# A fused patch, attention and expert kernel with its head rebuilt: gamma and beta spread by TensorE, attention weights first

## The reference

```python
parts = [x] + [_shift2d(x, HALF * s[2], HALF * s[0]) for s in shifts]
xc = jnp.concatenate(parts, axis=1)                      # 15 channels
patches = ... .reshape(B, h * w, p * p * C5)             # 3840 features a patch
mu = patches.mean(axis=-1, keepdims=True)
var = patches.var(axis=-1, keepdims=True)
xn = (patches - mu) * jax.lax.rsqrt(var + LN_EPS) * ln_gamma + ln_beta
return jnp.einsum('bnp,dp->bnd', xn, W) + b              # W: 192 x 3840
```

## Time and profile before

| | us |
|---|---|
| median of 3 runs | 677.99 (677.66 to 678.62) |
| the profiled execution, whole | 683.48 |
| its span in the profile | 681.7 |
| PE busy in the span | 543.7 (80%) |
| DVE, ACT, POOL busy | 406.0, 300.6, 198.3 |

### The profile page before, as it was taken

One profiled execution on the slowest core, in us unless ns is written; L12 is line 12 of the kernel. 1 busy time (PEld: TensorE's weight loads), 2 busy tenths in 40 slices (PEclk: granted clock), 3 DMA queues, 4 the chain that ended last, 5 costly groups with the idle time before them and its releaser, 6 DMA issues.

```text
span 681.7 us, 13237 instructions
## 1 busy us (share of the span) xinstructions
PE 543.7 (80%) x3330; PEld 504.9 (74%) x3331; DVE 406.0 (60%) x1343; ACT 300.6 (44%) x696; POOL 198.3 (29%) x293
## 2 busy tenths in 40 slices
PE   0079989997699999997019999999999999999300
PEld 0067688997497788886019999999999999999300
DVE  4590717666314789999715656565665656565297
ACT  0035991223523677876314444444544444444100
POOL 0001510000000267777702333333333333333300
PEclk9999997999579999998559999999999999999855
DMA  9999600000951022222222322222222222222398
GB/s 201 236 173 187 120 0 1 7 1 0 225 159 36 22 73 74 82 78 81 78 77 52 82 68 80 69 80 69 69 80 72 77 68 81 68 80 61 107 373 259
DMA packets 85235, 64.87 MB, mean 95 GB/s; under 512 B 42500, under 2 KB 81896, under 8 KB 84824
## 3 DMA queue, kind: packets, MB, share of 16 engines
q1 hardware_dynamic: 67160, 39.93, 26.4%
q0 software_dynamic: 8208, 16.95, 6.9%
q10 hardware_dynamic: 9840, 7.67, 3.9%
HBM read 42.61 MB, written 21.86 MB: 95 GB/s over the span
## 4 chain that ended last, share of the span: by engine, by line
PE 65%; DVE 15%; ACT 8%; DMA 6%; issue 3%; SPq 2%; ACTq 1%; POOL 0%; POOLq 0%; DVEq 0%
PE pair L736 9%; PE bank L931 5%; PE bank L927 5%; PE bank L928 4%; PE bank L930 4%; PE bank L929 4%; PE bank L938 4%; DVE hres L1334 4%; ACT sqjunk L463 4%; PE pair L947 4%; PE bank L947 4%; DMA bet<-in_L_tok_ln_beta 3%; PE pair L916 3%; PE pair L806 3%; PE bank L687 3%
## 5 line engine op out<-in xcount | busy, mean ns | idle before, releaser
L648 POOL DMA_INDIRECT disp<-xf,posu x82 | 79.7, 972 | 166.6 <-DVE posu L1212 142.0
L660 POOL DMA_INDIRECT ydram<-ysb,dnow x89 | 87.3, 981 | 69.4 <-POOL dnow L657 67.1
L1310 DVE TENSOR_TENSOR hh<-sg,bank 128x384 f32<-128x384 f32 x89 | 49.3, 554 | 84.0 <-ACT sg L601 84.0
L601 ACT ACTIVATE sg<-bank 128x384 f32<-128x384 f32 x89 | 43.7, 491 | 110.9 <-PE bank L931 110.9
L736 PE MATMUL pair<-wcT,imgT 128*128 128x193 f32 x432 | 74.7, 335 | 3.3 <-DVE tmp L1048 3.3
L736 PEld LDWEIGHTS pair<-wcT,imgT 128*128 128x128 f32 x432 | 73.7, 196 | 3.5 <-issue 3.5
L927 PE MATMUL bank<-wa,xh 128*128 x178 | 67.5, 379 | 0.0
L931 PE MATMUL bank<-wa,xl 128*128 x178 | 60.0, 337 | 0.0
L928 PE MATMUL bank<-wa,xh 128*128 x178 | 60.0, 337 | 0.0
L929 PE MATMUL bank<-wa,xl 128*128 x178 | 59.8, 336 | 0.0
L930 PE MATMUL bank<-wa,xh 128*128 x178 | 59.7, 335 | 0.0
(11 more groups left out here) (229 smaller groups left out, 1258.0 us busy)
## 6 DMA issues: line engine op xcount, KB each, us to landing
xs<-disp SPq DMA_DIRECT2D x89, 96.0 KB, 2.0
img<-in_x SPq DMA_DIRECT2D x12, 392.0 KB, 8.3
yall<-ydram SPq DMA_DIRECT2D x5, 768.0 KB, 13.9
yall<-ydram ACTq DMA_DIRECT2D x5, 768.0 KB, 15.0
hres<-in_txt SPq DMA_DIRECT2D x4, 768.0 KB, 13.2
xs<-disp SPq DMA_DIRECT2D x89, 33.5 KB, 1.9
wraw<-in_L_tok_W SPq DMA_DIRECT2D x1, 2880.0 KB, 17.0
raw_gu<-in_L_ffn_gate_w SPq DMA_DIRECT2D x7, 288.0 KB, 10.7
```

The costliest lines, as they stand in the source:

```text
L648: pool.indirect_dma_start(disp, bass.IndirectOffsetOnAxis(ap=posu[c % XBUF][:, 2 * j + k:2 * j + k + 1], axis=0), xfd[c % XBUF][:, j, :], None
L660: pool.indirect_dma_start(ydram, bass.IndirectOffsetOnAxis(ap=dnow[b][:], axis=0), ysb[b][:], None).then_inc(s_ys[b], 16)
L1310: v.tensor_tensor(hh[o][:], sg[o][:], bank[2 * o + 1][:, 0:DE], ALU.mult).then_inc(s_hh, 1)
```

## The change

- `gamma` and `beta` come as one row each into `gb1` on one partition. PE multiplies them by a column of ones (`onesf`, K = 1) in 8 pieces of 480 columns each, and ACT copies each piece from PSUM to `gam` or `bet` (`spread(n)`, 16 pieces, four banks). Pieces 0 to 7 stand first in PE's and ACT's streams, pieces 8 to 15 behind the 16 attention products.
- SP now issues gamma, beta, the four attention weights, `wraw` in two halves and the image. ACT issues only the constants and small parameters.
- The products use four banks; ACT copies `gT`, DVE copies `hT`.
- DVE zeroes nothing of the image any more (POOL does), makes the small tables and centres `wq` first, and then waits for all 16 spread pieces before the gamma multiply, which goes to a new tile `wsc`. The folds are made in `wsc`, counted by `s_wsc`; PE's weight transposes wait for them alone. The beta sums come after the folds.
- POOL waits for `s_wprep` and cuts strips 0, 2, 4, 5, 6, 7; DVE cuts 1 and 3 (`strip_out`).
- Of image groups 0 to 15 DVE copies the even ones and ACT the odd ones. ACT's eight copies stand ahead of `squares(0)`.
- `patch_out(p)` waits for `s_sq` at 2p+2 and no longer for 18.
- The text load is split in two (after the weight transposes, after the squares), and the groups of `stats1` are in another order.

```diff
         @block.sync
-            sp.dma_start(wraw[:], W.rearrange("(m p) f -> p m f", p=DH)).then_inc(s_wraw, 16)
-            sp.dma_start(bet[:], beta.partition_broadcast(DH)).then_inc(s_bet, 16)
-            sp.dma_start(gam[:], gamma.partition_broadcast(DH)).then_inc(s_gam, 16)
+            for k, w in enumerate((gamma, beta)):
+                sp.dma_start(gb1[:, PFEAT * k:PFEAT * k + PFEAT], w.unsqueeze(0)).then_inc(s_gb, 16)
+            sp.dma_start(wq[:], w_query.rearrange("(c p) d -> p c d", p=P)).then_inc(s_attw, 16)
...
+            for m in range(2):
+                sp.dma_start(wraw[:, m, :], W[DH * m:DH * m + DH, :]).then_inc(s_wraw[m], 16)
...
         @block.scalar
+            def spread(n):
+                act.wait_ge(s_gbm, n + 1)
+                to = (gam, bet)[n // 8]
+                nc.scalar.copy(to[:, 480 * (n % 8):480 * (n % 8) + 480], bank[4 + n % 4][0:DH, 0:480]).then_inc(s_gbo, 1)
...
-            act.wait_ge(s_wprep, 1)
+            for g in range(1, 16, 2):
+                act.wait_ge(s_it, g + 1)
+                nc.scalar.copy(imgT[:, g // 4, g % 4, :, :], bank[3 + g % 2][:, 0:CH * P].rearrange("p (c t) -> p c t", c=CH)
+                               ).then_inc(s_ita, 1)
...
         @block.gpsimd
+            pool.wait_ge(s_wprep, 1)
             pool.wait_ge(s_img, 16 * 12)
             pool.wait_ge(s_border, 1)
-            for r in range(8):
+            for r in (0, 2, 4, 5, 6, 7):
...
         @block.tensor
+            def spread(n):
+                if n >= 4:
+                    pe.wait_ge(s_gbo, n - 3)
+                pe.matmul(bank[4 + n % 4][0:DH, 0:480], onesf[:], gb1[:, 480 * n:480 * n + 480], start=True, stop=True
+                          ).then_inc(s_gbm, 1)
...
-            pe.wait_ge(s_wprep, 1)
+            for n in range(8, 16):
+                spread(n)
+            pe.wait_ge(s_wsc, 8)
             for g in range(12):
...
         @block.vector
+            v.wait_ge(s_gbo, 16)
+            for m in range(2):
+                v.wait_ge(s_wraw[m], 16)
+                st.link(v.tensor_tensor_reduce(wsc[:, m, :], wraw[:, m, :], gam[:], 1.0, 0.0, ALU.mult, ALU.add,
+                                               colsum[:, 0, m:m + 1]))
...
+            for m in range(2):
+                st.link(v.tensor_tensor_reduce(wraw[:, m, :], wraw[:, m, :], bet[:], 1.0, 0.0, ALU.mult, ALU.add,
+                                               colsum[:, 1, m:m + 1]))
...
             def patch_out(p):
-                v.wait_ge(s_sq, 18)
+                v.wait_ge(s_sq, 2 * p + 2)
...
+            strip_out(1)
+            for g in range(0, 16, 2):
+                if g == 8:
+                    strip_out(3)
                 img_out(g)
```

More of the change, by code:

```diff
@@ L304, in part_of @@
             return (1 if s == 0 else 3) if dr <= 0 else (4 if s == 0 else 2)
-        wv5 = wraw[:].rearrange("p m (y x c) -> p m y x c", y=16, x=16)
+        wv5 = wsc[:].rearrange("p m (y x c) -> p m y x c", y=16, x=16)
         def pipeline(eng, step, parts, ahead, peel=0):
@@ L362, in _ @@
                                      x[:, c, 40 * ih:40 * ih + 56, 40 * jh:40 * jh + 56]).then_inc(s_img, 16)
-            sp.wait_ge(s_wprep, 1)
+            sp.wait_ge(s_wt, 12)
             for q in range(TQ):
-                sp.dma_start(hres3[32 * q:32 * q + 32, PTILES:TILES, :], txt_q[q]).then_inc(s_txt, 16)
+                sp.dma_start(hres3[32 * q:32 * q + 32, PTILES + 8:TILES, :], txt_q[q][:, 8:]).then_inc(s_txt[0], 16)
+            sp.wait_ge(s_sq, 18)
+            for q in range(TQ):
+                sp.dma_start(hres3[32 * q:32 * q + 32, PTILES:PTILES + 8, :], txt_q[q][:, 0:8]).then_inc(s_txt[1], 16)
             sp.wait_ge(s_it, 32)
@@ L629, in _ @@
                                pattern=[[1, P]], channel_multiplier=-1).then_inc(s_cons, 1)
+            for ih in range(2):
+                pool.wait_ge(s_pool, 4 + 3 * ih)
+                pool.memset(img[64 * ih:64 * ih + 64, :, 56 * ih:56 * ih + 8, :], 0.0).then_inc(s_pool, 1)
+                for jh in range(2):
+                    a, r0 = 64 * ih + 32 * jh, 8 - 8 * ih
+                    pool.wait_ge(s_pool, 5 + 3 * ih + jh)
+                    ins = pool.memset(img[a:a + 32, :, r0:r0 + 56, 56 * jh:56 * jh + 8], 0.0)
+                    if not (ih and jh):
+                        ins.then_inc(s_pool, 1)
+            ins.then_inc(s_border, 1)
+            pool.wait_ge(s_wprep, 1)
             pool.wait_ge(s_img, 16 * 12)
             pool.wait_ge(s_border, 1)
-            for r in range(8):
+            for r in (0, 2, 4, 5, 6, 7):
                 if r >= 2:
@@ L670, in _ @@
         def _(pe):
+            def spread(n):
[3 more added lines that the diff above has]
+                          ).then_inc(s_gbm, 1)
+            pe.wait_ge(s_pool, 1)
+            pe.wait_ge(s_gb, 32)
+            for n in range(8):
+                spread(n)
             pe.wait_ge(s_cons, 1)
@@ L683, in _ @@
                 h, o = n // 2, 64 * (n // 2 % 2)
-                pe.wait_ge(s_eg, n + 1 if n else 2)
+                pe.wait_ge(s_ega, 2)
+                if n >= 4:
+                    pe.wait_ge(*((s_egd, (n - 3) // 2) if n % 2 else (s_ega, n // 2 + 1)))
                 lhs, rhs = (wk, wq) if n % 2 == 0 else (wv, woT)
                 for m in range(2):
-                    ins = pe.matmul(bank[n % 2][0:DH, D * m:D * m + D], lhs[o:o + 64, h // 2, DH * m:DH * m + DH],
+                    ins = pe.matmul(bank[n % 4][0:DH, D * m:D * m + D], lhs[o:o + 64, h // 2, DH * m:DH * m + DH],
                                     rhs[o:o + 64, h // 2, :], start=True, stop=True)
                 ins.then_inc(s_pg, 1)
-            pe.wait_ge(s_wprep, 1)
+            for n in range(8, 16):
+                spread(n)
+            pe.wait_ge(s_wsc, 8)
             for g in range(12):
                 if g == 0:
-                    pe.wait_ge(s_eg, 2 + 2 * NH)
+                    pe.wait_ge(s_ega, 2 + NH)
+                    pe.wait_ge(s_egd, NH)
                 if g >= 2:
@@ L718, in img_t @@
             def img_t(g):
-                if g >= 2:
-                    pe.wait_ge(s_itout, g - 1)
+                if 2 <= g < 18:
+                    pe.wait_ge((s_itd, s_ita)[g % 2], g // 2)
+                elif g >= 18:
+                    pe.wait_ge(s_itd, g - 9)
                 r, m = g // 4, g % 4
-                pe.wait_ge(s_strip, r + 1)
+                if r in (1, 3):
+                    pe.wait_ge(s_strip1, r // 2 + 1)
+                else:
+                    pe.wait_ge(s_strip, r // 2 + 1 if r < 4 else r - 1)
                 for c in range(CH):
@@ L728, in patch @@
                 i, j = p // 3, p % 3
-                pe.wait_ge(s_itout, min(32, 8 * i + 16))
+                pe.wait_ge(s_itd, 8 * i + 8)
+                pe.wait_ge(s_ita, 8)
                 if p == 0:
@@ L961, in _ @@
             st = Steps(v, s_dve)
[L963 to L1000, removed]
             v.wait_ge(s_rw8, 32)
@@ L1015, in _ @@
             st.mark(v.memset(zrow[:], 0.0))
+            v.wait_ge(s_attw, 64)
+            st.link(v.tensor_reduce(wqm[:], wq[:], AX.X, ALU.add))
+            st.link(v.tensor_scalar(wqm[:], wqm[:], 1.0 / D, None, ALU.mult))
+            v.tensor_tensor(wq[:], wq[:], wqm[:].unsqueeze(2).to_broadcast([P, 4, D]), ALU.subtract).then_inc(s_wqc, 1)
+            for n in range(1, 2 * NH, 2):
+                v.wait_ge(s_pg, n + 3)
+                v.tensor_copy(hT[:, :, n // 2, :], bank[n % 4][0:DH, 0:384].rearrange("p (m d) -> p m d", m=2)
+                              ).then_inc(s_egd, 1)
+            v.wait_ge(s_gbo, 16)
[4 more added lines that the diff above has]
+            for m in range(2):
+                for dr in range(2):
+                    for s in range(2):
+                        px, ox = (8, 0) if s == 0 else (0, 8)
+                        y0 = 8 * ((dr + 1) % 2)
+                        k = CH * part_of(dr, s)
+                        dst = wv5[:, m, y0:y0 + 8, px:px + 8, k:k + CH]
+                        v.tensor_tensor(dst, dst, wv5[:, m, 8 * dr:8 * dr + 8, ox:ox + 8, 0:CH], ALU.add).then_inc(s_wsc, 1)
+            for m in range(2):
+                st.link(v.tensor_tensor_reduce(wraw[:, m, :], wraw[:, m, :], bet[:], 1.0, 0.0, ALU.mult, ALU.add,
+                                               colsum[:, 1, m:m + 1]))
+            v.wait_ge(s_par, 16 * 5)
+            st.mark(v.tensor_tensor(colsum[:, 1, :], colsum[:, 1, :], biasc[:], ALU.add))
+            st.wait()
+            v.memset(vb[:], 1.0).then_inc(s_wprep, 1)
+            v.wait_ge(s_wprep, 1)
+            for k in range(2):
+                for m in range(2):
+                    st.mark(v.tensor_scalar(vb[:, k, m, :], vb[:, k, m, :], colsum[:, k, m:m + 1], None, ALU.mult))
+            st.wait()
             v.memset(ecs[:], 0.0).then_inc(s_vb, 1)
@@ L1064, in stats1 @@
                 if g == 0:
-                    v.wait_ge(s_txt, 64)
```

(17 more changed lines are left out.)

44 lines of the change are left out of this document (25 added, 19 removed).

## The result

The changed kernel takes 690.6 us (689.3 to 691.3, 4 runs) against 678.2 (677.7 to 678.6, 4 runs): a ratio of 1.018 (95% interval 1.016 to 1.020), 12.4 us slower. The forecast was 697.5 with a range of 684 to 704: right in direction and in the place that decides, 7 us too high, with one term of its sum wrong by 9 us.

The account below looks back on a forecast made before the run. It took the head, up to patch 3's start, to bound the kernel: patch 3 16.9 us late plus 3.0 for the clock, sum +19.9, taken as +19.5 on the median 677.99, gives 697.5 us; range 684 to 704.

Parts of the forecast that it names:

- the place that decides: Squares after ACT's eight copies, at 87.0 us; first root at 123.2 holds DVE, making patch 3 16.9 us late.
- Patches 0 to 2 under the squares: With the relaxed wait, PE runs patches 0, 1 and 2 from about 88 to 115 us while ACT does squares.
- the head without slack: A change of the head is worth what it does to the start of patch 3, plus the clock's effect there.
- A spread at 1.6 us: Each 480-column spread on PE takes 1.6 us at half clock; eight gamma or eight beta pieces take 12.8 us.
- The products: The 16 attention products on PE take 18.0 us less 0.3 for four banks and second copy engine, ending at 36.4.
- DVE's strip: DVE's strip 1, three copies before its first image copy, takes 1.8 us, with bounds 1.0 and 2.2.
- The clock at patch 3: After PE idles some 15 us, patch 3 runs partly at half clock, adding 3.0 us.
- rival (a): Spreads on PE run at full clock, 0.8 us each, saving 12.8 us: 684.7 us; chance 0.08.
- signs that I had named for being wrong: Spread records of 0.4 us, first square before 80 us, or patch 3 following patch 2 without a long pause.
- (b): The whole head runs at full clock, patch 3 is 5.1 us early: 672.9 us, faster than before; chance 0.05.
- (c): ACT is late for the first spread, each us beyond 9.5 shifting everything by one: 700 to 706 us; chance 0.09.
- (d): The gain is real but its end hides it, since squares are not what ends last; no separate chance given.

Follow-up runs that it names:

- run with the squares first: Changed kernel with ACT copying no image groups and DVE all of them, PE's waits on the copies put back; 673.0 us, ratio to before 0.992.
- split wait: Changed kernel with the first half of the gamma multiply waiting for the 8 gamma pieces alone: 686.9 us; with DVE also copying all image groups: 668.6 us.
- two-bank run: Changed kernel with the 16 attention products waiting as if there were two banks; 703.0 us.
- run with the relaxed wait: Kernel before with only patch_out(p) waiting for its own squares instead of all; 677.9 us, ratio 0.998.
- the second trace: Kernel before, unchanged, profiled anew; 679.5 us median, span of this trace 677.7.

## Why the prediction was right, and where its size was off

**The place that decides: right.** It was squares behind ACT's eight copies, the first root behind all squares, DVE held in `patch_out(0)`, group 24 and patch 3 behind DVE. From the first square to patch 3 I had 46.2 us and measured 46.1 (77.2 to 123.3). The run with the squares first shows it by taking it away: 17.6 us.

**Patches 0 to 2 under the squares, and the head without slack: right.** Patch 2 ended at 104.9 with the squares running to 111.8, and the split wait gave 3.7 and 4.4 us, where its multiply is 4.2.

**A spread at 1.6 us, at half clock: right.** Records of 480 columns take 999 ns at half clock and 561 at full; eight gamma pieces took 13.1 us against 12.8. Only the first two beta pieces ran at full clock, which the products had left until 30.3 us, and beta took 11.3 instead of 12.8.

**The products: the step that failed.** I took 18.0 us from the earlier trace rows and allowed 2 us at most for four banks, taking 0.3. They took 8.9. The two-bank run gives 18.9 back and the four-bank run on the kernel before has them in 9.5: the banks set it. So the step of the prediction that failed is the overlap that it gave the four banks, 0.3 us where they were worth 9, and with it the half clock that it kept for all products. Heads alternate between rows 0 to 63 and rows 64 to 127 of the array, and with a free bank the products of one head run beside those of the next. The changed kernel shows the pairs (timeline of PE):

```profile
21.02 0.52 PE L730 MATMUL bank<-woT,wv 64*96 64x192 f32 x1
21.02 0.63 PE L730 MATMUL bank<-wq,wk 64*96 64x192 f32 x1
21.34 0.52 PE L730 MATMUL bank<-woT,wv 64*96 64x192 f32 x1
21.45 0.52 PE L730 MATMUL bank<-wq,wk 64*96 64x192 f32 x1
...
24.00 0.32 PE L730 MATMUL bank<-woT,wv 64*96 64x192 f32 x1
24.08 0.32 PE L730 MATMUL bank<-wq,wk 64*96 64x192 f32 x1
```

There are two starts every 0.32 us instead of one, and from 23.5 us on, when the granted clock rises, two every 0.16 us. The gain has two parts. At half clock two products side by side take 1.4 us (21.02 to 22.42); the first and the last product have no partner, so that sixteen make nine such steps, 12.5 us. This is an estimate from these rows; by it 5.5 us of the 18.0 go by the overlap and 3.6 more by the clock. The trace of before held the hint (ACT's copies: start, length, what, wait):

```profile
41.04 0.47 ACT L449 COPY gT<-bank 96x384 f32<-96x384 f32 x1 [2.10 <-PE bank L687]
42.32 0.47 ACT L449 COPY hT<-bank 96x384 f32<-96x384 f32 x1 [0.81 <-PE bank L687]
43.19 0.47 ACT L449 COPY gT<-bank 96x384 f32<-96x384 f32 x1 [0.40 <-PE bank L687]
```

The copies come 1.28 and 0.87 us apart in turn, and the shorter step is where the row half changes: with two banks the products already overlapped there by 0.4 us. The Trainium skill (TensorE: Matmul & The Clock Gate, Part 3) says that matmuls with few rows run at the same time when their operands lie in distinct row groups; by it this term would have been some 11.5 us at half clock, nine steps of four records of 0.32 us, which is an estimate. These rows agree that they run side by side, at 1.4 us a step.

**DVE's strip: 1.1 us instead of 1.8**, inside the bounds. `vb` took 1.1 us more than in the kernel before (2.0 to 0.9 for its four multiplies). POOL cuts its first strip in just that time (DVE then POOL in the changed kernel: start, length, what), as it did not before; that the two hinder each other I have not tested.

```profile
60.22 2.02 DVE L1063 TENSOR_SCALAR vb<-vb,colsum 96x128 f32<-96x128 f32 x4
```
```profile
60.24 1.72 POOL L669 COPY strip<-img 128x512 f32<-128x512 f32 x3 [50.17 <-DVE vb L1059]
```

**The clock at patch 3: less than half of the price.** The pause was 16.4 us and the clock did fall, at 108.9. It rose 3.9 us after PE's restart at 122.0; in the kernel before it took 6.1 after 103.4. Patch 3 took 9.1 us, not 11.1. In the run with the relaxed wait it rose 6 us after the restart and patch 3 took 10.1. The run with half of the multiply earlier and the one with two banks have the same instructions here and the same pause of 16.4 us; there the clock rose 3.2 and 2.8 us after the restart, and patch 3 took 8.8 and 8.5. So the price of a restart at half clock was between 0.7 and 3.2 us in these traces, over the 7.88 us of a patch at the full clock, and it differs between kernels that do the same at this place. What sets it is not shown.

**The sum.** Patch 3 came 9.9 us before its forecast: 8.8 by the products, 1.5 by the beta pieces, 0.7 by the strip and 0.9 by the image groups, against 1.0 for a later start of the products and 1.1 for `vb`. The clock in the patches took 1.8 less. Against that stand 2.4 us behind the patches, which I had at 0 (the 1.7 and 0.7 above), and 1.0 because patch 3 of the kernel before is at 115.3 in the second trace. Together this is 8.3, from the 19.9 of the sum to the 11.6 between the traces.

**What the prediction's own signs say.** PE's pause of 12 to 18 us (16.4), half clock at the start of patch 3 and spread records near 0.8 us all came, though a spread record is written with 1.0 us where the starts are 0.8 apart. But products over by 36 us (28.6), weight transposes near 60 (51.1), squares near 87 (77.2) and a first root near 123 (113.4) came 8 to 10 us early, and one of the signs that I had named for being wrong is there: a first square before 80 us. It is there because the products were 9 us shorter, while the squares still ended last, so the sign spoke of the size and not of the place. The range was in part luck: the small terms reached down to 697.5 - 6 = 691.5, and 690.6 lies inside only because I had widened the range to reach rival (a), which did not come.

**The rivals.** (a), spreads at full clock, did not come. (b) fell: the clock was at half from 30.3 to 71.3 us. (c) fell: ACT had its small DMAs issued by 4.9 us and was through with its table load at 6.2. (d) fell: the squares did end last, as the run with the squares first shows.

## What to carry to other kernels

Read an engine's stream as a queue: a copy given to a less busy engine, ahead of long work that someone else waits for, moves that work by the whole time the copy waits, not by the time it takes. Here eight copies of 0.48 us pushed 34.7 us of squares back by 17 us (from 60.2 to 77.2), and the rest of the change was a gain of 5.6 us hidden behind them. A relaxed wait is worth only what the next wait on the same engine leaves of it. And where small matmuls use half of the array's rows, look at their banks: two more of them let the products run side by side, the clock rose with it, and together that halved their time.

## What the runs showed of the hardware

- The page's granted clock reads 1.00 where nothing has been recorded yet. Durations tell the level: 524 ns to 322 for a record of 192 columns with K = 64, 999 to 561 for 480 columns with K = 1, 421 to 272 for a 128x128 transpose.
- With two banks, where products of the two row halves overlap by some 0.4 us in 2.2, the clock stayed at half for 18 us (kernel before) and 18.9 us (two-bank run). With four banks, where they run side by side, it was full after 3.9 us (changed kernel, 19.7 to 23.5) and 5.2 us (four banks on the kernel before, 38.7 to 43.9). Thirteen us of K = 1 matmuls did not raise it, and 9.5 us of them ran at half after it had fallen.
- In the kernel before the clock rose to full at 75.4 us, when PE had done only fp32 image transposes since 68.9; in the changed one at 71.3, with transposes alone since 64.7. The Trainium skill (TensorE: Matmul & The Clock Gate, Part 4) has it that the full clock does not engage for TensorE's transpose mode; here it did under the kernel's transposes, and the measurement decides for them. Whether they run in the mode that the page means, no trace shows: the profile records them as matmuls with the identity.
- The kernel before lay between 676.6 and 684.1 us, the one with the squares first between 671.9 and 674.9. Of 4.0 us between two traces of the kernel before, 3.3 are one more stretch of half clock in the work on keys; that the rest of the spread is of this kind was not traced.
